# Q projections in a phase of their own ahead of the attention heads, two weight tiles a head, and each wait issued once

## The reference

```python
# x: 4 x 2048 x 2048, 16 heads of 128
qkv  = einsum('bsd,ed->bse', x, w_qkv) + b_qkv        # split into q, k, v by heads
attn = softmax(q @ k.T / sqrt(128) + causal, axis=-1)
x    = layernorm(x + (attn @ v) @ w_out.T + b_out)
g, u = x @ Wg.T, x @ Wu.T                             # 8192 x 2048, (uint8 - 128) * scale
x    = layernorm(x + (silu(g) * u) @ Wd.T)            # Wd 2048 x 8192, the same way
```

## Time and profile before

| | us |
|---|---|
| median of 2 runs | 3462.28 (3447.87 to 3476.69) |
| the profiled execution | 3453.28 |
| its slowest core, 7, first to last instruction | 3451.7 |
| its fastest core, 2 | 3432.5 |
| PE, ACT, DVE busy on core 7 | 2541.7, 1081.7, 907.6 |

### The profile page before, as it was taken

One profiled execution on the slowest core, in us unless ns is written; L12 is line 12 of the kernel. 1 busy time (PEld: TensorE's weight loads), 2 busy tenths in 40 slices (PEclk: granted clock), 3 DMA queues, 4 the chain that ended last, 5 costly groups with the idle time before them and its releaser, 6 DMA issues.

```text
span 3451.7 us, 35798 instructions; the slowest of 8 cores (3432.5 to 3451.7 us)
## 1 busy us (share of the span) xinstructions
PE 2541.7 (74%) x12224; PEld 1133.4 (33%) x12224; DVE 907.6 (26%) x1908; ACT 1081.7 (31%) x1678; POOL 63.2 (2%) x117
## 2 busy tenths in 40 slices
PE   0767666666676667629419999988865999998882
PEld 0333333333333333314104444433322444443330
DVE  0132323323333333331242222211113222221112
ACT  0233333333333333330243333322232333332222
POOL 1000000000000000000000000000001000000001
PEclk9888888888888888859659999989987999999995
DMA  7111111111111000044222222211114222221113
GB/s 125 19 19 19 19 19 19 19 19 19 19 19 19 13 18 14 7 122 68 12 19 79 78 75 78 75 55 55 55 26 109 77 76 77 77 67 55 55 49 55
DMA packets 46126, 164.06 MB, mean 48 GB/s; under 512 B 5888, under 2 KB 6016, under 8 KB 45952
## 3 DMA queue, kind: packets, MB, share of 16 engines
q1 hardware_dynamic: 29808, 103.04, 11.6%
q0 software_dynamic: 16144, 58.73, 8.7%
HBM read 193.21 MB, written 8.39 MB: 58 GB/s over the span
## 4 chain that ended last, share of the span: by engine, by line
PE 63%; issue 11%; DVE 9%; ACT 8%; POOLq 3%; DMA 3%; DVEq 2%; ACTq 1%; POOL 0%; SPq 0%
PE OPp L736 14%; PE SB L658 13%; PE SB L661 13%; PE SB L250 12%; PE SB L552 3%; ACT AWa L363 3%; ACT AWa L379 3%; POOLq L227 2%; PE OPp L412 2%; DVE wbf L719 2%; PE SB L335 2%; DVE AWa L401 2%; PE PTa L389 2%; DMA mbc<-m_row 1%; DMA rbc<-r_row 1%
## 5 line engine op out<-in xcount | busy, mean ns | idle before, releaser
L658 PE MATMUL SB<-AWa,wbf 128*128 128x512 bf16 x2048 | 779.2, 380 | 105.0 <-ACT wbf L631 52.6
L250 PE MATMUL SB<-AXa,wbf 128*128 128x512 bf16 x2560 | 691.6, 434 | 194.6 <-POOLq L227 192.4
L661 PE MATMUL SB<-AWa,wbf 128*128 128x512 bf16 x2048 | 779.0, 380 | 0.0
L736 PE MATMUL OPp<-AXa,wbf 128*128 128x512 bf16 x2048 | 497.2, 408 | 107.9 <-DVE wbf L719 98.2
L250 PEld LDWEIGHTS SB<-AXa,wbf 128*128 128x128 bf16 x2560 | 270.6, 109 | 587.1 <-issue 381.6
L363 ACT ACTIVATE AWa<-AWa,negm 128x512 f32<-128x512 f32 (+1 forms) x320 | 214.1, 670 | 688.0 <-DVEq L358 688.0
L736 PEld LDWEIGHTS OPp<-AXa,wbf 128*128 128x128 bf16 x2048 | 210.2, 104 | 394.9 <-issue 189.5
L658 PEld LDWEIGHTS SB<-AWa,wbf 128*128 128x128 bf16 x2048 | 201.0, 98 | 349.7 <-issue 109.7
L661 PEld LDWEIGHTS SB<-AWa,wbf 128*128 128x128 bf16 x2048 | 200.9, 98 | 243.2 <-issue 3.1
L677 DVE SCALAR_TENSOR_TENSOR AXa<-SB,usc_s,gsb 128x512 bf16<-128x512 f32 x128 | 96.1, 751 | 656.0 <-ACT gsb L672 656.0
L713 ACT ACTIVATE wbf<-stg,c 128x2048 bf16<-128x2048 uint8 x64 | 127.9, 2002 | 435.4 <-PE OPp L736 419.9
(11 more groups left out here) (74 smaller groups left out, 1214.7 us busy)
## 6 DMA issues: line engine op xcount, KB each, us to landing
stg<-wgu SPq DMA_DIRECT2D x128, 512.0 KB, 3.6
stg<-wd SPq DMA_DIRECT2D x64, 512.0 KB, 3.8
wbf<-wqkv POOLq DMA_DIRECT2D x48, 512.0 KB, 5.2
AXa<-xkv POOLq DMA_DIRECT2D x16, 512.0 KB, 29.7
AXa<-xq POOLq DMA_DIRECT2D x1, 8192.0 KB, 28.4
wbf<-wout POOLq DMA_DIRECT2D x16, 512.0 KB, 5.2
yt<-AZa POOLq DMA_DIRECT2D x32, 256.0 KB, 3.9
mbc<-m_row SPq DMA_DIRECT2D x4, 256.0 KB, 11.2
```

The costliest lines, as they stand in the source:

```text
L250: e.matmul(SB[:, b * 512:(b + 1) * 512], wbf[wb_i][:, dc * 128:(dc + 1) * 128], rhs, start=(dc == 0), stop=(dc == NDC - 1)))
L658: e.matmul(SB[:, gb:gb + 512], wbf[sg_][:, dc * 128:(dc + 1) * 128], rr, start=(dc == 0), stop=(dc == NDC - 1)))
L661: e.matmul(SB[:, ub:ub + 512], wbf[su_][:, dc * 128:(dc + 1) * 128], rr, start=(dc == 0), stop=(dc == NDC - 1)))
L736: e.matmul(OPp[:, ob: ob + 512], wbf[q % 4][:, (ic % 16) * 128:(ic % 16) * 128 + 128], Hbuf[:, ic * 512:(ic + 1) * 512], start=(ic == 0), ...
```

## The change

- A loop over the 16 heads ahead of everything else loads each Q weight tile, runs its 32 matmuls into two banks and takes them away on ACT. It has the form of the output projection's loop.
- `kv_dma` loads K and V alone, into `wbf[(2hh)%4]` and `wbf[(2hh+1)%4]`; `proj_unit_mm` and `proj_unit_evac` lose the Q case; the units ahead of the loop are 8 and not 10; blocks 6 and 7 have one unit.
- `W` remembers for each engine and semaphore the highest value that was waited for, and leaves a wait out when it asks for no more than that. This holds for the whole kernel.

```diff
+    _wait_hwm = {}
+
     def W(eng, sem, val):
         assert val <= sem.n, (eng, sem.name, val, sem.n)
         if val <= 0:
             return
+        key = (eng, sem.name)
+        if _wait_hwm.get(key, -1) >= val:
+            return
+        _wait_hwm[key] = val
         E(eng, lambda e, s=sem, v=val: e.wait_ge(s.h, v))
...
-        q_evac_done = 0
+        for fc in range(NH):
+            need("gpsimd", f"wbf{fc % 4}")
+            W("gpsimd", dG, dG.n)
+            I("gpsimd", dG, lambda e, fc=fc: e.dma_start(
+                wbf[fc % 4][:],
+                wqkv_d.ap()[fc].rearrange("p c f -> p (c f)")), 16)
+            I("gpsimd", eG, lambda e: e.drain())
+            W("tensor", dG, dG.n)
+            W("tensor", eG, eG.n)
+            if fc >= 2:
+                W("tensor", eS, ev_tok[fc - 2])
...
+            for dc in range(NDC):
+                for th in range(2):
+                    bank = (fc % 2) * 2 + th
...
+                         e.matmul(SB[:, bank * 512:(bank + 1) * 512],
+                                  wbf[fc % 4][:, dc * 128:(dc + 1) * 128], rhs,
+                                  start=(dc == 0), stop=(dc == NDC - 1)))
...
+            W("scalar", eT, mm_tok)
+            for th in range(2):
+                bank = (fc % 2) * 2 + th
+                I("scalar", eS, lambda e, fc=fc, th=th, bank=bank: e.activation(
+                    QT[:, fc * 1024 + th * 512: fc * 1024 + th * 512 + 512],
+                    SB[:, bank * 512:(bank + 1) * 512],
+                    AF.Identity, bias=bqs[:, fc:fc + 1], scale=QK_SCALE))
+            ev_tok[fc] = eS.n
+        q_evac_done = eS.n
...
         def kv_dma(hh):
-            qb, kb, vb = (3 * hh) % 4, (3 * hh + 1) % 4, (3 * hh + 2) % 4
-            need("gpsimd", f"wbf{qb}")
-            W("gpsimd", dG, dG.n)
-            I("gpsimd", dG, lambda e, hh=hh, qb=qb: e.dma_start(
-                wbf[qb][:], wqkv_d.ap()[hh].rearrange("p c f -> p (c f)")), 16)
-            qd = dG.n
-            I("gpsimd", eG, lambda e: e.drain())
-            qt_ = eG.n
+            kb, vb = (2 * hh) % 4, (2 * hh + 1) % 4
...
-        for u in range(10):
-            mtok, b, kind, tc = proj_unit_mm(0, u)
-            proj_unit_evac(0, u, mtok, b, kind, tc)
+        for u in range(8):
+            mtok, b, isv, tc = proj_unit_mm(0, u)
+            proj_unit_evac(0, u, mtok, b, isv, tc)
...
-                    if kc == 0:
-                        W("tensor", eS, qt_done[h][j // 4])
+                    if h == 0 and j == 0 and kc < 2:
+                        W("tensor", eS, q_evac_done)
...
                 if h + 1 < NH:
                     u_mm = proj_unit_mm(h + 1, j)
-                    u_mm2 = proj_unit_mm(h + 1, 15 - j) if j >= 6 else None
...
                     proj_unit_evac(h + 1, j, *u_mm)
-                    if u_mm2 is not None:
-                        proj_unit_evac(h + 1, 15 - j, *u_mm2)
```

More of the change, by code:

```diff
@@ L187, in build_nc @@
         W("scalar", eV, tok_memset)
-        q_evac_done = 0
+        for fc in range(NH):
[9 more added lines that the diff above has]
+                W("tensor", eS, ev_tok[fc - 2])
+            if fc == 0:
+                W("tensor", eV, tok_memset)
+            for dc in range(NDC):
+                for th in range(2):
+                    bank = (fc % 2) * 2 + th
+                    rhs = Xbkv[:, dc * 2048:(dc + 1) * 2048].rearrange(
+                        "p (a b f) -> p a b f", a=8, b=2)[:, th * 4:(th + 1) * 4, 0:1, :]
+                    f = (lambda e, fc=fc, dc=dc, bank=bank, rhs=rhs:
+                         e.matmul(SB[:, bank * 512:(bank + 1) * 512],
+                                  wbf[fc % 4][:, dc * 128:(dc + 1) * 128], rhs,
+                                  start=(dc == 0), stop=(dc == NDC - 1)))
+                    if dc == NDC - 1 and th == 1:
+                        I("tensor", eT, f)
+                    else:
+                        N("tensor", f)
+            used(f"wbf{fc % 4}", eT)
+            mm_tok = eT.n
+            if fc == 0:
+                ev_tok = {}
+            W("scalar", eT, mm_tok)
[7 more added lines that the diff above has]
+        q_evac_done = eS.n
         tap("qt", QT[:, :], eS, q_evac_done)
@@ L201, in build_nc @@
         kvinfo = {}
-        qt_done = {}
         kt_ready = {}
@@ L228, in kv_dma @@
             vt_ = eG.n
-            kvinfo[hh] = (qb, kb, vb, qd, qt_, kd, kt_, vd, vt_)
+            kvinfo[hh] = (kb, vb, kd, kt_, vd, vt_)
             kt_ready[hh] = [None] * 4
-            qt_done[hh] = [None, None]
         def proj_unit_mm(hh, unit):
-            qb, kb, vb, qd, qt_, kd, kt_, vd, vt_ = kvinfo[hh]
+            kb, vb, kd, kt_, vd, vt_ = kvinfo[hh]
             b = 2 + (unit % 2)
[L236 to L241, removed]
+            is_v = unit < 4
+            tc = unit if is_v else unit - 4
+            wb_i = vb if is_v else kb
+            if is_v:
+                W("tensor", dG, vd)
+                W("tensor", eG, vt_)
+            else:
+                W("tensor", dG, kd)
+                W("tensor", eG, kt_)
             W("tensor", eS, unit_evac[unit % 2])
             for dc in range(NDC):
[L244 to L249, removed]
+                f = (lambda e, wb_i=wb_i, dc=dc, b=b, tc=tc:
                      e.matmul(SB[:, b * 512:(b + 1) * 512],
                               wbf[wb_i][:, dc * 128:(dc + 1) * 128],
-                              rhs, start=(dc == 0), stop=(dc == NDC - 1)))
+                              Xbkv[:, dc * 2048 + tc * 512: dc * 2048 + tc * 512 + 512],
+                              start=(dc == 0), stop=(dc == NDC - 1)))
                 if dc == NDC - 1:
@@ L261, in proj_unit_mm, with proj_unit_evac @@
                 used(f"wbf{kb}", eT)
[L262 to L266, removed]
+            return eT.n, b, is_v, tc
+        def proj_unit_evac(hh, unit, mm_tok, b, is_v, tc):
             W("scalar", eT, mm_tok)
-            if kind == "v":
+            if is_v:
                 need("scalar", f"stg{tc // 2}")
@@ L274, in proj_unit_evac @@
                 vt_ready[hh] = eS.n
-            elif kind == "k":
+            else:
                 need("scalar", f"kt{hh % 2}")
@@ L281, in proj_unit_evac @@
                 kt_ready[hh][tc] = eS.n
[L282 to L287, removed]
             unit_evac[unit % 2] = eS.n
```

## The result

| | us |
|---|---|
| before, lowest of 10 runs | 3445.43 |
| after, lowest of 11 runs | 3393.95 |
| after, median | 3396.24 |
| after, the profiled execution: spans of core 7 and of the slowest core, 1 | 3390.5, 3392.4 |
| ratio of the times, 95% interval | 0.983, 0.980 to 0.986 |

The kernel became 1.7% faster, which is clear of the noise and under 2%. The forecast was 3397.

The account below looks back on a forecast made before the run. It took each attention block to be set by the later of PE's unit and the DVE/ACT softmax chain, the unit being late in block 0. Terms -132 - 13 + 35 - 36 - 2 + 92 = -56 from 3453.3 gave 3397 us, range 3358 to 3435.

Parts of the forecast that it names:

- Head starts: Block 0 of each head: PE no longer waits for late weight tiles, 8.8 us times 15, -132 us.
- Double units: Blocks 6 and 7: with one projection unit instead of two, PE is no longer late, -13 us.
- The clock: Blocks 6 and 7: less PE work lets its granted clock fall, 2.3 us a head, +35 us.
- The clock that holds: Rival, 20%: PE's clock in blocks 6 and 7 does not fall, +35 becomes near 0, total 3362 us.
- Waits: Every attention block: repeated waits on PE and DVE left out, 0.27 us a block, -36 us.
- The front: Ahead of the heads: 512 Q matmuls in 112.6 us, PE starting at 66.5, delay head 0 by +92 us.
- the waits in the shadow: Rival, 10%: second waits hide behind the first, so -36 becomes about -5, total 3428 us.
- late tiles: Rival, 2%: weight tiles still come late at head starts, total 3529 us.
- a slow front: Rival, 6%: the Q matmuls ahead of the heads run at 8.7 us a tile, total 3423 us.
- half clock throughout: Rival, 5%: PE at half clock throughout the head loop, units late in blocks 0 to 5, about 3600 us.
- The clock that falls in every block 6 and 7: Rival, 12%: PE's clock falls in blocks 6 and 7 of every head, +78 instead of +35, 3440 us.

Follow-up runs that it names:

- e3: The kernel before with six weight tiles in the loop instead of four, Q still in the loop, all waits kept: 3343.5 us against 3445.4, ratio 0.969.
- e1: The changed kernel with every left-out wait issued again, all else unchanged: 3430.0 us against 3394.0.
- e9: The changed kernel with 16 more matmuls, whose result is overwritten, ahead of the unit of block 7 alone: 3379.2 us.
- e4: The kernel before with six weight tiles and each wait issued once, Q still in the loop: 3291.3 us, ratio 0.953.
- e2: The kernel before with each wait issued once, Q units in the loop and four tiles kept: 3407.0 us against 3445.4, ratio 0.987.
- e6: The changed kernel with two more, already satisfied, waits ahead of the transposes of every block: 3422.3 us.

## Why the prediction was right, term by term

- **Head starts**, -132. In the means over all cores block 0 lost 8.6 us, of which 0.3 are its waits, and in head 0 12.1: 14 x 8.3 + 11.8 = **-128**. Right in size and place; the earlier trace rows and the new block 0 show it, and e3 shows it alone with 127.
- **Double units**, -13. The transposes came 0.62 us late in block 6 and 0.15 in block 7 before (means over heads 1 to 14, beyond a handover), and not at all after: 0.77 x 15 = **-12**. The reading behind it was off: 10 of the 30 double units of core 7 stood at 7.07 us, a third and not half.
- **The clock**, +35. What is left of the change in blocks 1 to 7 when lateness and 0.27 us of waits a block are taken off is 0.2 in blocks 1 to 5, 0.5 in block 6 and 1.1 in block 7: 1.8 x 15 = 27. Against e1, which has all waits as before, it is 1.3 + 0.77 = 2.1 a head, or 31. So about **+30**. The clock that holds (20%) did not come: 0.75 and 0.72 in blocks 6 and 7. e9 got back half of it. Head 14's block 6 at 1.00 was not typical of the kernel before: on core 7 it was so in 6 of 15 heads. And in one point the argument went wrong: I took the clock for something that only the missing double units change. e3 kept them and still lost 25 us outside block 0. Yet most of the +30 does belong to the moved Q units, as e4 against the changed kernel shows, since neither has the stall and both have each wait once. The changed kernel is 0.81 us a head longer in the loop (79.90 against 79.09), although 0.94 us of lateness is gone from it (0.77 in block 6, 0.08 in block 7, 0.09 in block 1): 1.75 x 15 = 26.
- **Waits**, -36. **-36** by e1, -38 by e2, and 0.11 us each by e6.
- **The front**, +92. 113.5 us for the 512 matmuls on core 7 (112.6 busy on core 1) against 112.6 taken over from the earlier trace rows, 67.06 against 66.5 for the start, and 1.5 us that I did not have: the first unit waits for the last Q bank to be taken away (1.51 <-ACT AZa L227). 210.8 - 115.5 = **+95**.
- Sum: -128 - 12 + 30 - 36 - 2 + 95 = -53, and 3453.3 - 53 = 3400 against 3394 to 3396 measured. The errors of single terms, at most 5 us, went both ways.

The front ran at 113.5/512 = 0.222 us a matmul on core 7, as the earlier trace rows had it, and on each of the eight cores the granted clock was 1.00 from 67 to 180 us. The Trainium skill ("TensorE: Matmul & The Clock Gate", "Part 1: The HAM clock gate") states 13/16 of the clock for dense matmuls on three or more cores of a die. By an estimate from that rule the front would have taken about 138 us; here the trace does not agree with the page.

The rivals: the waits in the shadow are refuted by e1 and e6; late tiles and a slow front by the rows above; half clock throughout by block 1, at 1.00 in 10 of 15 heads of core 7. The clock that falls in every block 6 and 7 came true in part: 1.6 of the 5.2 us a head that full half clock would cost.

What the change as a whole does is best read from e4. The tiles and the waits alone bring 154 us. Moving Q ahead of the loop was one way to need only two tiles a head, and it cost 103 of them: by the rows 95 for work that had mostly been hidden behind the softmax chain and now stands in the open, and 0.8 us a head, 12 in all, in the loop (107 against the 103 measured).

## What to carry to other kernels

Work that hides behind another engine's chain costs little (0.85 us a head in late double units here), and a phase of its own turns it into span; where a ring of buffers is too short, look for room for more buffers before moving the work. Price each wait in front of a bounding instruction, satisfied or not: some 0.1 us each on PE, and 36 us in all here. And sum a change from its blocks, each against its own bound, because a stall that is removed may have been hiding other things.

## What the hardware showed that I had not expected

- A wait that is already satisfied costs PE's sequencer 0.11 us when it stands directly ahead of the work, each time and in addition (28 us for 256 of them in e6).
- Matmuls whose result is thrown away made the kernel faster: 240 of them, 3.5 us a head of added work, took 15 us off (3394.0 to 3379.2), and some 16 off the median core of a die.
- Removing the wait for the tile, with 8.2 us of lateness at each head's start, made blocks 1, 2, 6 and 7 of the same head 1.7 us longer in all (e3), at unchanged work.
